# The eight early maxima products of an attention layer on two pairs of PSUM banks

## What is computed

```python
x = x + 0.5 * _L0_ffn_ref(_layernorm(x), ...)
x = x + _L0_attn_ref(_layernorm(x), W_qkv, W_o)         # alibi bias
x = x + 0.5 * _L0_ffn_ref(_layernorm(x), ...)
x = x + 0.5 * _L1_ffn_ref(_layernorm(x), ...)
x = x + _L1_attn_ref(_layernorm(x), Wq, bq, ..., bo)    # rotary positions, biases
x = x + 0.5 * _L1_ffn_ref(_layernorm(x), ...)
# attention: softmax(q k^T / sqrt(16) + bias, causal) v, then the output projection
```

## Time and profile before

| | us |
|---|---|
| median of 3 runs | 1671.06 (1669.83 to 1676.87) |
| profiled execution, its own time | 1678.49 |
| its span, first to last instruction | 1676.7 |
| mean granted clock of TensorE in it | 0.942 of 2.4 GHz |
| TensorE busy with matmuls | 1521.5 (91%) |
| VectorE busy | 1243.0 (74%) |
| ScalarE busy | 945.6 (56%) |
| maxima reductions on VectorE (L1348, 640 of them) | 665.3 |

### The profile page before, as it was taken

How to read it: one execution, slowest core, us unless ns; L and a number is a source line. 1 busy time by engine, 2 the same in 40 slices (tenths; PEclk the granted TensorE clock), 3 DMA queues, 4 the chain that set the end, 5 groups by cost and what they waited for, 6 DMA issues and landing times. The chain is left out here.

```text
span 1676.7 us, 32231 instructions
## 1 busy us (share of the span) xinstructions
PE 1521.5 (91%) x13116; PEld 950.9 (57%) x13116; DVE 1243.0 (74%) x1741; ACT 945.6 (56%) x1893; POOL 207.6 (12%) x275
## 2 busy tenths in 40 slices
PE   2798878999999999999899698999999999998997
PEld 0687754444434445688688576544344344456886
DVE  7765457888898883575588886687788988635897
ACT  5454334758768887565344322455577788763442
POOL 0243000000000000166001032000000001120000
PEclk9998968999999999999899897698799999999999
DMA  5000959000000000200100066841110000000000
GB/s 216 26 0 10 182 151 129 26 25 21 19 14 13 2 2 2 76 1 1 38 1 1 15 134 192 101 62 43 30 42 25 13 12 2 2 1 1 13 13 26
DMA packets 38195, 70.58 MB, mean 42 GB/s; under 512 B 5490, under 2 KB 13298, under 8 KB 37236
## 3 DMA queue, kind: packets, MB, share of 16 engines
q1 hardware_dynamic: 38052, 68.58, 18.0%
HBM read 48.90 MB, written 22.15 MB: 42 GB/s over the span
## 5 line engine op out<-in xcount | busy, mean ns | idle before, releaser
L1348 DVE TENSOR_REDUCE l_att_maxima<-psum 128x2 f32<-128x1024 f32 (+3 forms) x640 | 665.3, 1063 | 150.6 <-PE psum L1140 142.2
L1533 ACT ACTIVATE l_att_probs<-psum 128x512 f32<-128x512 f32 (+3 forms) x1280 | 603.8, 533 | 267.1 <-PE psum L1170 246.5
L1187 PE MATMUL psum<-l_att_probs,l_att_v 128*17 128x256 f32 (+2 forms) x4608 | 354.1, 384 | 0.5
L1170 PE MATMUL psum<-l_att_qt,l_kt 51*128 51x512 f32 (+6 forms) x1280 | 321.1, 464 | 6.7 <-ACT l_att_probs L1533 6.7
L1140 PE MATMUL psum<-l_kt,l_att_qt 59*128 59x512 f32 (+7 forms) x1280 | 289.5, 431 | 5.2 <-DVE l_att_maxima L1348 3.4
L1170 PEld LDWEIGHTS psum<-l_att_qt,l_kt 59*128 59x128 f32 (+1 forms) x1280 | 138.7, 193 | 157.7 <-ACT l_att_probs L1533 148.2
L1187 PEld LDWEIGHTS psum<-l_att_probs,l_att_v 128*17 128x17 f32 x4608 | 81.7, 96 | 144.6 <-issue 91.5
L1140 PEld LDWEIGHTS psum<-l_kt,l_att_qt 59*128 59x128 f32 (+1 forms) x1280 | 141.7, 204 | 19.4 <-DVE l_att_maxima L1348 17.7
L358 PE MATMUL psum<-xh,w_ternary 128*128 128x512 f32 x256 | 104.0, 406 | 21.0 <-PEq L165 16.3
L1137 PE MATMUL psum<-tri 64*128 64x128 bf16 x1024 | 90.4, 242 | 22.0 <-DVE l_att_maxima L1348 16.3
L1488 POOL CAST l_att_crow<-l_att_cneg 128x16 bf16<-128x16 f32 x32 | 8.1, 253 | 814.9 <-DVE l_att_cneg L1358 814.9
(11 more groups left out here) (209 smaller groups left out, 2477.9 us busy)
## 6 DMA issues: line engine op xcount, KB each, us to landing
l_kt<-qk_scratch SPq DMA_DIRECT2D x48, 256.0 KB, 10.0
qk_scratch<-l_att_kv_parts SPq DMA_DIRECT2D x22, 512.0 KB, 7.9
l_att_qt<-qk_scratch SPq DMA_DIRECT2D x168, 64.0 KB
qk_scratch<-y SPq DMA_DIRECT2D x10, 512.0 KB, 12.9
set_raw<-in_w_gu SPq DMA_DIRECT2D x2, 1024.0 KB, 6.9
y<-in_w_gu SPq DMA_DIRECT2D x1, 2048.0 KB, 7.6
y<-in_rope SPq DMA_DIRECT2D x8, 256.0 KB, 5.8
l_att_w_raw<-in_w_gu SPq DMA_DIRECT2D x4, 512.0 KB
```

Source lines behind the costliest of these rows:

```text
L1170: e.matmul(g.ps[:, score_bank(i), off:BLK], g.kt[rows_of(x), hp, kt * P:(kt + 1) * P], qt[rows_of(x), hp, off:BLK], start=u >= TPB, stop=True,
L1187: ins = e.matmul(g.ps[h * VW:h * VW + HD + 1, OB, lo:hi], g.v[:, kt, STEPS[st][1] * HG + h, :], pr[:, un % PB, h, lo:hi], start=u == 0 and ...
L1348: e.tensor_reduce(mp[:, st % 2, 2 * p:2 * p + 2, t, c], g.ps[:, bank:bank + 2, 0:w], AX.X, ALU.max).then_inc(s.mx, 1)
L1533: e.activation(pr[:, un % PB, h, off:BLK], g.ps[:, score_bank(i), off:BLK], ACT.Exp, scale=HD ** -0.5).then_inc(s.ex, 1)
```

## The change

In the last projection block the products k = 2, 4 and 6 write banks 2 and 3 instead of 0 and 1 (`early_bank`). k = 0, 1, 3, 5 and 7 stay in banks 0 and 1. The waits follow: k = 1 still waits for the maximum of k = 0; k = 2 waits only until VectorE has read the projection tiles that were last in banks 2 and 3 (`third_pair_read`); k = 3 to 7 wait for the maximum of k - 2 instead of k - 1. The first slot of the ring (bank 3 is in it) waits also for `mx` = 7, that is for the maximum of k = 6. `maxima` reads each product in its own pair. The number of products, reductions and transfers and their order on each engine stay the same.

```diff
+    def third_pair_read(e):
+        if rope:
+            e.wait_ge(s.za, 2 * (NM * NB - 1))
+        else:
+            e.wait_ge(s.r1, NM * (NB - 1) + 2)
...
+        def early_bank(k):
+            return 2 if k >= 2 and k % 2 == 0 else 0
...
             def open_slot():
                 if free[ring % 2] is not None:
                     e.wait_ge(*free[ring % 2])
                 elif ring:
                     kv.values_read(e)
                 else:
                     kv.pairs_read(e)
+                    e.wait_ge(s.mx, mbase[1] - 1)
                 return slot_bank(ring)
...
                 own = bank is None
                 if own:
                     bank = open_slot()
+                elif k == 2:
+                    kv.third_pair_read(e)
                 elif k:
-                    e.wait_ge(s.mx, k)
+                    e.wait_ge(s.mx, k if k == 1 else k - 1)
...
             def first_products(i):
                 for k in ahead(i):
-                    max_products(k, 0)
+                    max_products(k, early_bank(k))
...
             def first_maxima(i):
                 for k in ahead(i):
-                    maxima(k, 0)
+                    maxima(k, early_bank(k))
```

More of the change, by code:

```diff
@@ L690 @@
 Projections = namedtuple("Projections", "tensor scalar vector gpsimd sync load_k queries_stored parts_stored keys_loaded "
-                         "pairs_read values_read")
+                         "pairs_read third_pair_read values_read")
 def projections(nc, g, name, rope, a, sb, splits, small):
@@ L960, in projections @@
     return Projections(tensor, scalar, vector, gpsimd, sync, load_k, queries_stored, parts_stored, keys_loaded,
-                       pairs_read, values_read)
+                       pairs_read, third_pair_read, values_read)
 def attention_phase(nc, g, name, rope, a, qx, splits, small, loads=()):
```

## The result

The changed kernel took 1666.7 us in the median of 12 runs (1656.4 to 1675.3) beside 1677.6 for the kernel before: ratio 0.9939, 95% interval 0.9911 to 0.9966. By this ratio it is 10.2 us, where 6.0 was forecast. I pooled the runs of it with those of the kernel before (35 and 119; three that lay over 1.5% above the fastest of their series are left out): means 1668.0 and 1674.5, **6.5 us less, plus or minus 2.2** (1.96 standard errors).

A forecast was written before the change was run, and what follows sets the result against it. TensorE is busy for 91% of the span, and in the early stretches the end of the reduction of k = 7 sets what follows. 2.2 + 3.8 = 6.0 us off the 1671.1 median gives 1665.1 us, range 1658.5 to 1671.

The forecast's parts named there:

- The limit: Early products of each layer: the end of the reduction of k = 7 sets when everything later starts.
- Layer 1, 3.8 us: Layer 1's early products: the reduction of k = 7 ends at 1038.07 instead of 1041.91, 3.8 us earlier.
- B: Measuring distance in layer 1, from the start of the second early reduction (k = 1) to the negated row.
- Layer 0, 2.2 us: Layer 0's early products, at granted clock 0.50: the reduction of k = 7 ends 2.2 us earlier, 226.91 instead of 229.14.
- A: Measuring distance in layer 0, from the start of the first early reduction (k = 0) to the negated row.
- the first rival: Denser early stretch gets full clock: 5.0 instead of 3.8 us in layer 1, some 1.5 more in layer 0; chance 0.2.
- The new wait: k = 8 now waits for the reduction of k = 6: 0.4 us of TensorE, covered, costed at nothing.
- the half per cent: Whole kernel: time within 0.5% (8.4 us) of the kernel before, given a chance of 0.67.
- The load behind: Layer 0's steps: the 3.0 us wait for the second row's transfer moves with the steps and stays 3.0.
- Slower by the clock: Steps: alternating banks make TensorE's gaps short and many, more time at 1.2 GHz, 1676.3 us; chance 0.1.

The follow-up runs named there:

- fillers: Matmuls with unread results added in TensorE's two gaps before k = 0 and k = 1 of layer 0: ratio 0.9917 on the changed kernel, 0.9994 on the kernel before.

## Why the prediction was right

- **The limit.** The end of the reduction of k = 7 sets when the row comes, and the row sets the first scores: 7.53 or 7.54 us behind it in both kernels and layers. Shown.
- **Layer 1, 3.8 us.** Measured 4.0 (13.93 to 9.90). The step by which k = 3's reduction follows the last remainder held, by the run with k = 4 and 6 alone. The two B are not at one clock (0.54 and 0.74), but by the forecast's own working a clock that stays high up to k = 4 is worth only 0.2 us (3.6 to 3.8), and from k = 5 on the clock was 0.50 as assumed. The one miss: k = 4 waits 0.95 us, because the clock stayed up until then and it arrived early; the forecast had it arrive with the reduction. So TensorE waits 2.1 us in all there (0.95, 0.73 and 0.40), not about 1.
- **Layer 0, 2.2 us.** The banks are worth about 2.1 at equal mean clock. What failed is the assumption that the stretch keeps the granted clock of one profile, 0.50. A was 4.5 to 5.1 us shorter in the three profiles of the changed kernel, since the clock was 0.76 to 0.84 in them. That was the first rival's mechanism, priced at 1.5 us more; against the mean of the three one-pair stretches without fillers (15.60, 14.35, 13.84: 14.6) the changed kernel's three (mean 10.8) gain 3.8, so 1.7 above the banks'. So layer 0's row started at 224.65, not near 226.9, and layer 1's at 1032.45, not near 1035.9. In layer 1 the rival's 5.0 did not come: VectorE bound k = 4 and 5, and from k = 5 on the clock was low again.
- **The new wait.** Put at 0.4 us and covered; it was 0.76 in layer 0, where the higher clock brought TensorE there earlier, and 0.40 in layer 1, and the transposes still waited 1.83 and 1.4 us for GpSimd. Free, as said.
- **Sum and time.** 6.0 us worked out; about 4.0 + 2.1 = 6.1 by the banks, up to 7.8 with layer 0's clock; 6.5 plus or minus 2.2 timed over 35 runs, about half of it with a higher mean clock. So the times agree with the sum and do not prove it; it rests on the distances. The first series, 10.2 us or 0.61%, was above its own later ones; pooled it is 0.39%, inside the half per cent for which the forecast had its largest chance. 1666.7 lies within the range of 1658.5 to 1671, 1.6 from the forecast's 1665.1, but that closeness is luck: the forecast took off from 1671.1, a median of three runs, where 12 runs of the same kernel gave 1677.6, 6.6 us more, and the first series gained 4.9 us more in the medians than the 6.0 worked out. The two errors nearly cancel.
- **The load behind.** The wait for the second row did not stay 3.0; it was 1.7, 1.4 and 2.3 us in the three profiles of the changed kernel. It is no mark of the change: its longest was 0.8 to 3.0 in the four profiles with one pair in layer 0 and 0.2 to 3.4 in the others.
- **Slower by the clock** did not come. The Trainium skill's section "A second HAM failure mode: psum-queue depth-cycling" (page "TensorE: Matmul & The Clock Gate") tells of a kernel (bf16, 512 columns) that cycled through banks and lost throughput by a swinging clock. Here layer 0's stretch with two pairs had 0.62 to 0.84 of the clock and the one with a single pair 0.50 to 0.71, and layer 1's 0.73 to 0.74 against 0.54 to 0.60, so this case does not bear it out: fewer waits, not more, came with the second pair.

## What to carry to other kernels

When two engines take turns on one buffer, work the new order out instruction by instruction from the timeline: the gain is the shift of the last instruction that anyone waits for, which can be more than the waits removed (4.0 us for 3.5 in layer 1) where the other engine's idle time goes too. Look whether the two engines still wait for a third behind the stretch, and put work there: that and the change together gave 14 us, of which the distances account for 7 to 8. Judge an edit of a few us by distances between marks, at equal granted clock, before judging it by the time, and take the baseline from more than three runs where single runs spread over 20 us.

## What the runs showed of the hardware

The granted clock of the same stretch of code differed from profile to profile: with one bank pair and no fillers, layer 0's early stretch was granted 0.50, 0.62 or 0.71 and took 15.60, 14.35 or 13.84 us (three kernels that are alike up to there). The steps of layer 1 got between 0.91 and 0.96 and took 412.5 to 394.7 us, those of layer 0, with as many instructions of TensorE, VectorE and ScalarE (GpSimd has 60 there and 68 in layer 1), 392.9 to 396.5 in every profile. A busy TensorE did not by itself get the full clock: in the kernel before it worked from 1049.3 to 1073.7 us without a gap, at 0.50 throughout. Why layer 1's steps are the ones that lose the clock stays open.
